# Four late groups of a graph layer's gather, loaded row by row from SyncE

## The reference

```python
h = relu(layernorm(x))
p1 = tanh(h @ pp_W1 + pp_b1) @ pp_W2 + pp_b2
inter = concatenate([p1[src], p1[dst]], axis=-1) @ pi_W1 + pi_b1
inter = ((inter @ pi_W2 + pi_b2) @ pi_W3).reshape(E, 64, 8)
i1 = einsum('ecb,eb->ec', inter, edge_attr)
i1 = tanh(i1 @ ii_W1 + ii_b1) @ ii_W2 + ii_b2
out = x + segment_sum(i1, dst, 6250)
```

## Time and profile before

| what | value |
|---|---|
| time, median of 3 runs | 2023.58 us (2021.24 to 2024.89) |
| time of the profiled execution | 2023.63 us |
| its span, first to last instruction | 2021.8 us |
| PE matmul busy | 1745.8 us (86%) |
| DVE busy | 1442.2 us (71%) |
| ACT busy | 1097.3 us (54%) |
| POOL busy | 1492.9 us (74%) |
| mean granted clock of TensorE | 0.947 |

### The profile page before, as it was taken

One profiled execution on the slowest core, in us unless ns is written; L12 is line 12 of the kernel. 1 busy time (PEld: TensorE's weight loads), 2 busy tenths in 40 slices (PEclk: granted clock), 3 DMA queues, 4 the chain that ended last, 5 costly groups with the idle time before them and its releaser, 6 DMA issues.

```text
span 2021.8 us, 54864 instructions
## 1 busy us (share of the span) xinstructions
PE 1745.8 (86%) x19990; PEld 1142.2 (56%) x19990; DVE 1442.2 (71%) x1897; ACT 1097.3 (54%) x2401; POOL 1492.9 (74%) x1582
## 2 busy tenths in 40 slices
PE   7698888888888888888898898898888888888888
PEld 5465555555555555555565555555555555555666
DVE  7687777677676777677776777677767677667676
ACT  5565555555555555555555555555555555555554
POOL 3777777777777777777777777777777777777774
PEclk8799999999999999999999999899999999889999
DMA  6533333232332332323323323323233233222232
GB/s 138 124 69 61 55 61 62 55 61 55 61 61 55 62 62 55 60 56 63 61 56 61 61 55 62 60 56 62 55 61 63 56 61 61 56 55 58 57 70 47
DMA packets 261682, 126.82 MB, mean 63 GB/s; under 512 B 183545, under 2 KB 233704, under 8 KB 261432
## 3 DMA queue, kind: packets, MB, share of 16 engines
q1 hardware_dynamic: 210863, 74.12, 17.2%
q0 software_dynamic: 50048, 51.35, 14.6%
q10 hardware_dynamic: 646, 0.13, 0.0%
HBM read 119.47 MB, written 6.00 MB: 62 GB/s over the span
## 4 chain that ended last, share of the span: by engine, by line
POOL 68%; issue 22%; PE 6%; DMA 1%; DVE 1%; ACT 1%; SPq 1%; DVEq 0%; ACTq 0%; POOLq 0%
POOL u_rows L472 68%; PE bank L1173 2%; DMA u_rows<-u_tab,src_e 1%; PE bank L1156 1%; PE bank L1253 1%; PE spread_ps L1165 0%; PE bank L1180 0%; PE spread_ps L1027 0%; DMA x_sb<-x 0%; DVE o_sb L799 0%; ACT loc_rows L574 0%; PE bank L1148 0%; PE spread_ps L1015 0%; PE bank L1188 0%; SPq L356 0%
## 5 line engine op out<-in xcount | busy, mean ns | idle before, releaser
L472 POOL DMA_INDIRECT u_rows<-u_tab,src_e x1564 | 1486.4, 950 | 507.6 <-issue 475.1
L799 DVE TENSOR_TENSOR o_sb<-st_sb,spread_ps 128x2048 f32<-128x2048 f32 x391 | 893.1, 2284 | 429.2 <-PE spread_ps L1165 414.4
L617 ACT ACTIVATE st_sb<-bank,s_bias 64x256 f32<-64x256 f32 x1564 | 733.1, 469 | 479.3 <-PE bank L1156 462.8
L1173 PE MATMUL bank<-o_sb,g_sb 128*64 128x256 f32 x6256 | 821.8, 408 | 1.0 <-DVE o_sb L799 0.8
L1173 PEld LDWEIGHTS bank<-o_sb,g_sb 128*64 128x64 f32 x6256 | 438.7, 144 | 238.9 <-issue 46.2
L1156 PE MATMUL bank<-ident,u_rows 128*128 128x128 f32 x1564 | 286.4, 307 | 232.7 <-DMA u_rows<-u_tab,src_e 231.5
L1156 PEld LDWEIGHTS bank<-ident,u_rows 128*128 128x128 f32 x1564 | 210.0, 195 | 282.4 <-DMA u_rows<-u_tab,src_e 263.1
L871 DVE TENSOR_TENSOR hot_t<-loc_bc,bank 126x512 bf16<-126x512 bf16 x391 | 268.9, 688 | 127.5 <-PE bank L1253 83.3
L1253 PEld LDWEIGHTS bank<-hot,t_sb 128*65 128x65 f32 x3128 | 221.1, 142 | 154.1 <-issue 152.0
L605 ACT ACTIVATE tt_sb<-bank,z_bias 128x256 f32<-128x256 f32 x391 | 185.1, 473 | 190.6 <-PE bank L1173 190.6
L1253 PE MATMUL bank<-hot,t_sb 128*65 128x42 f32 x3128 | 268.1, 238 | 0.5 <-ACT t_sb L608 0.5
(11 more groups left out here) (115 smaller groups left out, 234.3 us busy)
## 6 DMA issues: line engine op xcount, KB each, us to landing
loc_bc<-loc_tab SPq DMA_DIRECT2D x391, 126.0 KB
u_rows<-u_tab,src_e POOLq DMA_INDIRECT x1564
v_win<-v_tab SPq DMA_DIRECT2D x391, 15.8 KB
basis<-edge_attr SPq DMA_DIRECT2D x24, 256.0 KB, 4.1
v_tab<-acc_all SPq DMA_DIRECT2D x6, 336.0 KB
u_tab<-basis SPq DMA_DIRECT2D x6, 224.0 KB
x_sb<-x SPq DMA_DIRECT2D x1, 1120.0 KB
src_e<-src SPq DMA_DIRECT2D x24, 32.0 KB, 3.3
```

Of the source, the lines that this page charges most:

```text
L472: pool.indirect_dma_start(out=u_rows[:, g % UR, j, :], out_offset=None, in_=u_tab[:, :], in_offset=bass.IndirectOffsetOnAxis(ap=src_e[:, g ...
L617: last = nc.scalar.activation(tiles[h * D:(h + 1) * D, j], s_ps[r][part].rearrange("p (q a e) -> p q a e", q=2, a=TILES), ACT.Identity, bi ...
L799: return nc.vector.tensor_tensor(o_sb[:, r, :, :].rearrange("p c (j e) -> p j c e", j=TILES), st_sb[:, r, :].rearrange("p (j e) -> p j e", ...
L1173: last = nc.tensor.matmul(z_ps[h * D:(h + 1) * D, 0:2 * P], g_sb[:, c, :], o_sb[:, r, c, 2 * h * P:(2 * h + 2) * P], start=(c == 0), stop= ...
```

## The change

The groups 320, 334, 347 and 358 (`SIDE`) are no longer gathered by POOL. SP loads their 2048 rows of u, one row by one DMA, into `side_u`, a part of `basis` whose attributes have been used by then. In each step from 12 (`SIDE_FROM`) on it reads six row numbers into registers with one instruction and issues six DMAs (`SIDE_ROWS`), until step 353. The row numbers come from `src` through four small loads into `dst_raw`. The starts of the windows, until now one read per step, come by one read of eight in every eighth step. For the four groups PE waits for `side_in` and not for `u_in`, and takes the rows from `side_u`. `LOOP_END` becomes 320, so that these steps are among those written out.

```diff
-    LOOP_END = Y_STEP // UN * UN
+    SIDE = (320, 334, 347, 358)
+    SIDE_FROM, SIDE_ROWS = 12, 6
+    LOOP_END = SIDE[0] // UN * UN
...
+        side_u = basis[:, 0:len(SIDE) * TILES * D].rearrange("p (s j d) -> p s j d", j=TILES, d=D)
+        side_src = dst_raw[0:1, :, :]
...
+            def load_side_src():
+                for s, g in enumerate(SIDE):
+                    sp.dma_start(side_src[:, s, :], src[g * GE:(g + 1) * GE].rearrange("(a e) -> a e", a=1)
+                                 ).then_inc(side_src_in, 16)
+            def starts_of(g):
+                return nc.values_load_multi_w_load_instructions(
+                    base_row[0:1, g:min(g + UN, NG)], [mybir.EngineType.SP], min_val=0, max_val=N - W)[1]
+            def side_rows(r, n):
+                s, e = divmod(r, GE)
+                if r == 0:
+                    sp.wait_ge(side_src_in, 16 * len(SIDE))
+                    sp.wait_ge(part1r, len(SIDE) * TILES * D // (PIECE * NBT))
+                rows = nc.values_load_multi_w_load_instructions(
+                    side_src[0:1, s, e:e + n], [mybir.EngineType.SP], min_val=0, max_val=N - 1,
+                    skip_runtime_bounds_check_because="src holds rows of x, as for the gathers")[1]
+                for i, at in enumerate(rows):
+                    p, j = divmod(e + i, TILES)
+                    sp.dma_start(side_u[p:p + 1, s, j, :], u_tab[bass.ds(at, 1), :]).then_inc(side_in[s], 16)
...
                 for n in range(NG):
                     if has(n):
                         g = n
+                        if g % UN == 0:
+                            starts = starts_of(g)
...
-                        start = sp.value_load(base_row[0:1, g:g + 1], min_val=0, max_val=N - W)
+                        start = starts[g % UN]
...
+                        r = (g - SIDE_FROM) * SIDE_ROWS
+                        end = min(r + SIDE_ROWS, len(SIDE) * GE)
+                        while 0 <= r < end:
+                            cut = min(end, (r // GE + 1) * GE)
+                            side_rows(r, cut - r)
+                            r = cut
...
-                    for j in range(TILES):
+                    for j in range(0 if g in SIDE else TILES):
...
-                    pe.wait_ge(u_in[u], n * (64 // UR) + 64)
-                    place_rows(u_rows[:, u, :, :], u % 2, False).then_inc(s_ready, 1)
+                    if last_pass and n + u in SIDE:
+                        s = SIDE.index(n + u)
+                        pe.wait_ge(side_in[s], 16 * GE)
+                        rows = side_u[:, s, :, :]
+                    else:
+                        aside = len([g for g in SIDE if g % UR == u and g < n + u]) if last_pass else 0
+                        pe.wait_ge(u_in[u], n * (64 // UR) + (64 - 64 * aside))
+                        rows = u_rows[:, u, :, :]
+                    place_rows(rows, u % 2, False).then_inc(s_ready, 1)
```

More of the change, by code:

```diff
@@ L66, in program @@
     Y_STEP = LATE_G + 6
-    LOOP_END = Y_STEP // UN * UN
+    SIDE = (320, 334, 347, 358)
+    SIDE_FROM, SIDE_ROWS = 12, 6
+    LOOP_END = SIDE[0] // UN * UN
     TURN = NG - 4
     assert EPP * NP == EARLY and LPP * NP == N - EARLY and LPP == 10 and Y_STEP + 4 * BATCHES < NG + 4
+    assert all(SIDE_FROM * SIDE_ROWS + (k + 1) * GE <= SIDE_ROWS * g for k, g in enumerate(SIDE)) and SIDE[-1] < FULL
     assert NP * NPP == N and PART * TILES + FULL * GE == E and F == FC * P and NG <= PIECE * PIECES
@@ L220, in program @@
         u_in = sems("u_in", UR)
+        side_src_in = sem("side_src_in")
+        side_in = sems("side_in", len(SIDE))
         v_in = sems("v_in", VR)
@@ L388, in store_rest @@
                 sp.wait_ge(stored, 128)
+            def load_side_src():
[16 more added lines that the diff above has]
+                    sp.dma_start(side_u[p:p + 1, s, j, :], u_tab[bass.ds(at, 1), :]).then_inc(side_in[s], 16)
             with sp.If(is_fast):
                 store_v()
+                load_side_src()
                 for n in range(NG):
```

## The result

The changed kernel takes 2329.08 us (median of 4 runs, 2328.66 to 2330.18), the kernel before 2024.24 in the same comparison: a ratio of 1.151, 95% interval 1.1495 to 1.1523. That is 305 us slower, where 149 had been forecast. The direction and the new bound were forecast; the loss is twice the forecast one, and the time lies just inside the forecast's own range of 2039 to 2331 us, 2 us under its upper end.

What follows compares the result with a forecast made beforehand. POOL's gathers bound the kernel at 5.0 us a step; SP was to become the bound at 5.55. Summed, 97.4 + 1898.1 + 3.5 + 156.7 + 16.0 = 2171.7 us of span, 2173 us of time, range 2039 to 2331.

Steps and rivals of the forecast that it cites:

- POOL's saved gathers: On POOL's queue: four groups fewer, 16 gathers x 1.254 = 20.1 us, all gained if POOL stays the bound.
- traffic: On the DMA queues: 2048 rows of 256 B are 0.5 MB beside 51.35 MB on POOL's queue; nothing taken.
- PE's longer written-out part: On PE: forty more steps written out and not looped, same matmuls; nothing taken for it.
- `loc_bc`, `v_win`, register work: In SP's step: the two loads with their register work and four gaps, 1.369 us.
- read of six row numbers: In SP's step: one read into registers, priced as the read of one start, 0.771 and a gap: 0.813 us.
- six rows: In SP's step: six DMAs at 0.276 us, with register work and gaps 0.482 each, 2.892 us together.
- starts: On SP: eight window starts in one read every eighth step, 0.370 us a step, where each step paid 1.08.
- src and basis: On SP: their loads every sixteenth step, 0.102 us a step.
- every word of a read costs: Rival on SP's reads: 0.158 us a further word adds 0.93 us; step 6.47 us, time 2490 us; chance 0.05.
- the case in which SP keeps up: Rival: SP's step 5.05 us or less, POOL stays the bound, 16 gathers saved; 2003.5 us; chance 0.30.
- The upper end: Top of the range: a row's DMA midway between 0.276 and 0.432, SP's step 6.01 us, time 2331 us.
- its sign of 0.28 or more: On SP, in the profile after: the issue of one row's DMA should take 0.28 us or more; wrong if under 0.2.

## Why the prediction was right and wrong

Right: that SP becomes the bound; that the loss is its step times 342, taken from the step's instructions one by one; that POOL's saved gathers are worth nothing then; and, on the chips that the kernel before ran on in 2023 to 2024 us, that traffic, PE's longer written-out part and DVE and ACT cost nothing (without the reads the full 20 us came). POOL waited for PE 163 times, not in nearly every group.

Wrong in the size, by one term above all:

| term, us a step | put in | measured |
|---|---|---|
| `loc_bc`, `v_win`, register work | 1.37 | 1.39 |
| read of six row numbers | 0.81 | (1.22 + 1.78) / 2 + 0.04 = 1.54 |
| six rows | 2.89 | 2.57 |
| starts | 0.37 | 0.37 |
| src and basis | 0.10 | 0.11 |
| sum | 5.55 | 5.97 |

The measured terms are means over the 342 steps, from each instruction's start to the next one's.

The step that failed is "one read of six row numbers into registers: nearest row the read of one start, 0.771". It put the price of one word in for six. The rival "every word of a read costs" came near to the size of this term (it put in 0.79 more, and 0.73 was measured), with a chance of only 0.05. As a mechanism it isn't right: eight words from a boundary took less than six, and the starts cost 0.37 us a step as forecast, where the rival had them dearer too. The dearer read was partly paid back by the rows, 0.32 us a step: the DMA of one row issues in 0.225 us, under the 0.276 that was called the cheapest seen. So 0.276 was no floor, and the case in which SP keeps up was nearer than it looked: with reads of 24 words it is what happens.

That the time still lies in the range is luck. The upper end was worked out for a dearer row DMA, and that one was cheaper; the read of six, whose price made the miss, was let vary only downwards. For the same reason the number that was to be read first, the issue of one row's DMA, was the wrong one to watch: with 0.225 us, under its sign of 0.28 or more, the forecast would have seemed too high.

Of the 156.7 us that the span is longer than forecast, (2146.05 - 103.10) - 1898.1 = 144.9 us are the step. The load of step 12 starts at 103.10 and not at 97.4, 5.7 us later. The four loads of row numbers and the first read of starts now stand ahead of all, and the first `loc_bc` load starts at 62.97 and not at 58.38; that this delay of 4.6 us carries through to step 12 is likely but not shown, and the last 1.1 us are open. From the `v_win` load of step 354 to the end it is 182.4 us where 3.5 + 156.7 + 16.0 = 176.2 were put in, 6.1 more. PE's placing of the groups 353 and 354, and the busy times and granted clock of the stretch before:

```profile
2149.95 0.71 PE L1196 MATMUL bank<-ident,u_rows 128*128 128x128 f32 x4
2154.05 0.71 PE L1196 MATMUL bank<-ident,u_rows 128*128 128x128 f32 x4
```

```profile
2142.00:2148.00 6.00, 6.00 (x48) 3.94 (x48) 4.46 (x5) 2.25 (x5) 2.34 (x3) 0.50 0.38 51
```

PE places group 354 at 2154.05, 8.0 us behind its `v_win` load and not 3.5. In the steps before, a placing stands 5.1 us behind its `v_win` load (median; 4.7 at the least), because the path from SP to PE goes by the other load: DVE waits for `loc_bc` (the 848.4 us above), makes `hot_t`, and PE comes after it. That is 1.6 of the 4.5 us. The other 2.9 came with PE's clock: PE waited 5.5 us until 2141.7, then was busy without a pause at a granted clock of 0.50, the 1.2 GHz level, and its step from group 352 to 353 took 6.4 us. So the lower level costs nothing while SP is the bound, as forecast (between 105 and 2140 us the granted clock was 0.90 in the mean and SP never waited), but it cost at the step in which PE took over. From there 36 steps take 158.2 us, 1.5 more than put in, and the end 0.1 more. PE's own pace in that part was right, 4.45 us between 2199.50 and 2203.96:

```profile
2199.50 0.71 PE L1196 MATMUL bank<-ident,u_rows 128*128 128x128 f32 x4
2203.96 0.71 PE L1196 MATMUL bank<-ident,u_rows 128*128 128x128 f32 x4
```

## What to carry to other kernels

An engine that only issues DMAs has a budget per step like any other: add up its instructions, reads of registers first, before it gets more work, and compare with the step of the engine that is the bound. Read register values in few, large reads that start on 16 bytes: four further words from such a boundary cost here about what one further word costs elsewhere (0.225 against 0.20 us). A mean wait is at most the room that a queue has: with 0.44 us a step of it, a row and a longer read that took 0.48 were too much. And the gain of 1.1% holds for the chip that it was measured on; on another the same kernel lost 17%.

## What the runs showed of the hardware

The price of a read from SBUF into SP's registers, behind the `v_win` load: 0.77 us for one word; 1.03 for eight words from a boundary, two pieces; 1.93 for 24, six pieces, which is (1.93 - 1.03) / 4 = 0.225 us a further piece. Six words from a boundary, 1.23, are then one piece (estimated, 1.03 - 0.225 = 0.81) and two single words at 0.21. Six words 8 bytes off, 1.77, are 0.77 and five more at 0.20. The Trainium skill ("Runtime: NRT & Kernel Launch", Instruction fetch mechanics) has about 200 ns a register, for loads from HBM even in bulk: by that rule, the single words here agree, and the pieces of four don't.

Place counts for about a quarter of a microsecond: the same read of six is that much cheaper behind a row's DMA (0.98 and 1.53 us) than behind the `v_win` load (1.23 and 1.78), and six words from a boundary take 0.73 us behind the read of the starts or the load of `basis`.

The DMA of one row of 256 B, with its address from a register, issues in 0.225 us, and with its register work and gaps it takes 0.41 to 0.43 us of the queue.
